# Strassen products for two column blocks of tiles 8 to 15, and a new order of all calls

## The reference, cut to what matters

```
x: (2, 1024, 2048) f32, ctx: (2, 2048, 2048) f32
q1 = fake_quant(layernorm(x)); q2 = fake_quant(ctx)     # (round(v/s + z) clipped to 0..255, - z) * s
x  = x + tanh(g_xattn) * (q1 @ q2)                      # main product, 1024 x 2048 x 2048 per batch
y  = layernorm(x)
logits = y @ route_w.T (8 experts); top-1 expert and its logit
h  = y @ A_e.T (rank 16); out = (logit * h of the top expert) @ Bw_e.T
x  = x + tanh(g_ffn) * out
```

## Time and profile before

| | |
|---|---|
| time of three runs | 363.27, 364.12, 364.35 us; median 364.12 |
| span of the profiled execution | 361.7 us, 2.4 us under the median |
| PE / DVE / ACT / POOL busy | 333.0 / 260.6 / 197.4 / 172.3 us |
| share of the span | 92 / 72 / 55 / 48 % |
| main matmuls of 512 columns, in the program | 1008, and 32 of 256 columns |

### The profile page before, as it was taken

How to read it: one execution, slowest core, us unless ns; L and a number is a source line. 1 busy time by engine, 2 the same in 40 slices (tenths; PEclk the granted TensorE clock), 3 DMA queues, 4 the chain that set the end, 5 groups by cost and what they waited for, 6 DMA issues and landing times.

```text
span 361.7 us, 5854 instructions
## 1 busy us (share of the span) xinstructions
PE 333.0 (92%) x2237; PEld 186.4 (52%) x2262; DVE 260.6 (72%) x553; ACT 197.4 (55%) x129; POOL 172.3 (48%) x199
## 2 busy tenths in 40 slices
PE   0389999999999999999998999999999999999983
PEld 0244454546756466455464546464464555465751
DVE  3855799898967896958658587945588567585853
ACT  1888489778967262747999270524062413204460
POOL 2559267431265162545999056627064441605281
PEclk9999999999999999999999999999999999999999
DMA  7999999895769998899799996666939890443956
GB/s 301 400 387 404 366 387 380 289 348 173 284 182 212 289 251 291 270 266 294 176 366 157 262 320 121 181 111 177 212 138 158 225 288 31 93 84 59 304 220 232
DMA packets 93906, 87.63 MB, mean 242 GB/s; under 512 B 71844, under 2 KB 72868, under 8 KB 89764
## 3 DMA queue, kind: packets, MB, share of 16 engines
q1 hardware_dynamic: 93856, 87.11, 79.5%
q10 hardware_dynamic: 12, 0.00, 0.0%
HBM read 52.49 MB, written 16.78 MB: 191 GB/s over the span
## 4 chain that ended last, share of the span: by engine, by line
PE 77%; DVE 8%; DMA 7%; issue 2%; ACT 2%; POOL 2%; ACTq 0%; SPq 0%; DVEq 0%
PE main L1575 46%; DMA xs<-in_x 4%; PE hp L1613 4%; PE hp L1617 4%; PE hp L1614 4%; PE outp L1575 4%; PE outp L1658 4%; PE outp L1660 3%; PE outp L1659 3%; DVE bn L971 3%; PE turn L1609 2%; DMA prow<-in_g_ffn 2%; DMA out<-xs 1%; ACT x L753 1%; PE turn L1503 1%
## 5 line engine op out<-in xcount | busy, mean ns | idle before, releaser
L1575 PE MATMUL main<-q,qa 128*128 128x512 bf16 x841 | 194.6, 380 | 5.0 <-POOL q L593 2.3
L1575 PEld LDWEIGHTS main<-q,qa 128*128 128x128 bf16 x864 | 83.2, 98 | 101.2 <-issue 2.7
L586 POOL TENSOR_TENSOR yn<-y,yn 128x2048 f16<-128x2048 f32 x13 | 53.0, 4077 | 31.7 <-ACT y L788 31.7
L735 ACT ACTIVATE c<-stage,zpc,inv 128x2048 int8<-128x2048 f32 x24 | 49.9, 2086 | 7.7 <-DMA stage<-in_ctx 4.0
L593 POOL CAST q<-c 128x2048 bf16<-128x2048 int8 x24 | 45.1, 1893 | 15.3 <-ACT c L735 14.8
L782 ACT ACTIVATE yn<-xs,sc 128x2048 f16<-128x2048 f32 x11 | 23.0, 2093 | 53.4 <-POOL sc L579 49.6
L1104 DVE SCALAR_TENSOR_TENSOR xs<-main,cc,xs 128x512 f32<-128x512 f32 x45 | 33.3, 740 | 21.7 <-PE main L1575 21.5
L574 POOL TENSOR_SCALAR ve<-mv 128x1 f32<-128x1 f32 x16 | 3.1, 191 | 84.8 <-DVE mv L1137 81.8
L1184 DVE SCALAR_TENSOR_TENSOR xs<-outp,tsc,xs 128x512 f32<-128x512 f32 x44 | 31.2, 735 | 13.6 <-PE outp L1660 13.5
L971 DVE BATCH_NORM_STATS2 bn<-xs 128x6 f32<-128x512 f32 x52 | 32.1, 680 | 10.6 <-DMA xs<-in_x 10.6
L753 ACT ACTIVATE x<-xs,sc 128x2048 int8<-128x2048 f32 x12 | 25.0, 2087 | 24.5 <-POOL sc L566 24.4
(11 more groups left out here) (132 smaller groups left out, 435.2 us busy)
## 6 DMA issues: line engine op xcount, KB each, us to landing
stage<-in_ctx SPq DMA_DIRECT2D x24, 1024.0 KB, 7.9
xs<-in_x SPq DMA_DIRECT2D x13, 1024.0 KB, 6.5
out<-xs SPq DMA_DIRECT2D x12, 1024.0 KB, 5.0
yT<-in_ctx SPq DMA_DIRECT2D x4, 1024.0 KB, 9.2
y<-in_ctx SPq DMA_DIRECT2D x4, 1024.0 KB, 10.1
c<-in_x SPq DMA_DIRECT2D x3, 1024.0 KB, 7.4
out<-c SPq DMA_DIRECT2D x3, 1024.0 KB, 7.3
c<-in_L_ffn_A SPq DMA_DIRECT2D x1, 1024.0 KB, 11.5
```

What stands on the lines that cost most here:

```text
L586: pool.tensor_tensor(yn[:, 1, :], y[:, :], yn[:, 0, :], ALU.subtract).then_inc(s_ylo_made, 1)
L735: act.activation(c8_of(piece), place(piece), ACT.Identity, bias=zpc[:, 1:2], scale=inv[:, 1:2])\
L1575: last = pe.matmul(bank_of(n)[:, :], q1T(t)[:, k, :], q2[:, nb, k, :], start=(k == 0), stop=(k == KC - 1))
```

## The change

Four things change.

First, the number formats: `q2`, `q1` and `qa`, and what transposes them, become f16 in place of bf16. All values are whole numbers of at most 128 in size, and sums of four of them stay exact in f16.

Second, tiles 8 to 15 are taken in pairs (8,9), (10,11), (12,13), (14,15). Column blocks 0 and 1 are still `main`. Blocks 2 and 3 of a pair are eight products of (128 rows x 1024 contracted) by (1024 x 512) before, and seven after, in the form of Strassen's scheme that shares sums. DVE makes four sums of halves of `q1T` for each pair (`make_sum`, 128x1024 f16, two SBUF operands), and once, for batch 1, four sums of the context (`make_t1` to `make_t4`, each in two halves of 128x2048 f16). A product is eight matmuls. Products 1, 6, 5, 3 run on in one PSUM bank (`turn0`), 7 and 4 in another (`turn1`), and 2 in a bank of `main`; DVE adds the bank to x after each, so that a pair has seven additions for these blocks instead of four, and PE may go on in a bank only when the addition has been made.

Third, buffers: `yn` holds one tile and not two; the low part of y is written over y itself (`y_low`), so `norm_full` of the next tile waits until `flip_low` has landed (`y_turned`). Tiles 11 and 12 have their homes in `stage`, since `c8` holds the context's sums. The last tile's y goes to `c8[0]`.

Fourth, all five lists are in a new order, in the first half too.

```diff
-HOME = [0, 7, 1, 2, 3, 4, 0, 1, 2, 3, 4, 6, 7, 0, 1, 2]
+HOME = [0, 7, 1, 2, 3, 4, 0, 1, 2, 3, 4, 8, 9, 0, 1, 2]
-        q2 = sb("q2", [P, NB, KC, NW], bf16)
+        q2 = sb("q2", [P, NB, KC, NW], f16)
-        yn = sb("yn", [P, 2, D], f16)
+        yn = sb("yn", [P, D], f16)
+        qs = sb("qs", [P, 3, HK, P], f16)
         def y_turned(t):
-            return s_ylo_made, YN.index(t) + 1
+            return s_yloT_loaded, 16 * (YN.index(t) + 1)
+ADDED = {1: (0, W0), 2: (0, W0), 3: (0, W0 + 1), 4: (1, W0), 5: (1, W0 + 1), 6: (1, W0), 7: (1, W0 + 1)}
+        def factor_b(i):
+            return {1: q2[:, W0, 0:HK, :], 2: q2[:, W0, HK:KC, :], 3: q2[:, W0 + 1, HK:KC, :], 4: c8h[2],
+                    5: c8h[1], 6: c8h[0], 7: q2[:, W0 + 1, 0:HK, :]}[i]
+        def factor_a(t, i):
+            return {1: q1T(t)[:, 0:HK, :], 2: q1T(t)[:, HK:KC, :], 3: qs[:, 1, :, :], 4: q1T(t + 1)[:, HK:KC, :],
+                    5: qs[:, 0, :, :], 6: qs[:, 1, :, :], 7: qs[:, 2, :, :]}[i]
+            def make_sum(t, j):                       # j = 1; 2, 3 and 4 alike
+                    dve.tensor_tensor(qs[:, 0, :, :], low[:, 0:HK, :], low[:, HK:KC, :], ALU.add)\
+                       .then_inc(s_sum_made[0], 1)
...
+            def make_t1(half):                        # make_t2, make_t3, make_t4 alike
+                dve.tensor_tensor(half_of(c8h[1], half), in_q2(LATE + half), in_q2(LATE - PIECES + half), ALU.subtract)\
+                   .then_inc(s_t1_made, 1)
...
+            def add_product(t, i):
+                n, (into, nb) = UNIT[t, f"m{i}"], block_of((t, f"m{i}"))
+                dve.wait_ge(s_main_done, n + 1)
+                dve.scalar_tensor_tensor(out=x_nb, in0=bank_of(n)[:, :], scalar=cc[:, :], in1=x_nb,
+                                         op0=ALU.mult, op1=ALU.add).then_inc(s_main_added, 1)
+                if COMPLETES[into, nb] == (t, f"m{i}"):
+                    bn_block(into, nb)
...
+            def product(t, i, run):
+                if run == 0:
+                    pe.wait_ge(s_main_added, bank_before(n) + 1)
+                for k in range(4 * run, 4 * run + 4):
+                    first = i in (1, 2, 7) and k == 0
+                    last = pe.matmul(bank_of(n)[:, :], factor_a(t, i)[:, k, :], factor_b(i)[:, k, :],
+                                     start=first, stop=(k == HK - 1), skip_group_check=i in (6, 5, 3, 4))
```

In DVE's list, from the first pair on:

```diff
+            make_sum(8, 1)
+            make_t1(0)
+            make_sum(8, 3)
+            make_sum(8, 2)
+            add_main(8, 1)
+            make_t1(1)
+            make_t3(0)
+            add_main(9, 0)
+            stats1(10)
+            add_main(9, 1)
+            add_product(8, 1)
+            make_t3(1)
+            make_t2(0)
+            make_t2(1)
+            make_t4(0)
+            make_sum(8, 4)
+            add_product(8, 2)
+            add_product(8, 7)
+            add_product(8, 6)
+            make_t4(1)
...
+            stats1(12)
+            make_sum(10, 1)
+            add_product(10, 1)
+            make_sum(10, 2)
```

In PE's list, the first pair:

```diff
+            product(8, 1, 0)
+            product(8, 1, 1)
+            product(8, 7, 0)
+            product(8, 2, 0)
+            product(8, 2, 1)
+            product(8, 7, 1)
+            product(8, 6, 0)
+            product(8, 6, 1)
+            h_rows_high(7)
+            h_rows_low(7)
+            expert_product(6, 3)
+            product(8, 4, 0)
+            product(8, 5, 0)
```

More of the change, by code:

```diff
@@ L268, in build @@
         turn = [bank("turn0"), bank("turn1")]
-        turnb = [t[:, :].bitcast(bf16) for t in turn]
+        turnb = [t[:, :].bitcast(f16) for t in turn]
         hp = bank("hp")
@@ L1873, in _ @@
             main(7, 0, 3)
+            h_rows_high(5)
+            h_rows_low(5)
+            main(7, 2, 0)
+            main(7, 1, 0)
+            main(7, 1, 1)
             main(7, 1, 2)
+            turn_wh(5)
+            main(7, 2, 1)
+            main(7, 2, 2)
             main(7, 1, 3)
-            main(7, 2, 0)
-            expert_product(4, 2)
-            main(7, 2, 1)
+            expert_product(5, 0)
+            expert_product(5, 1)
+            main(7, 2, 3)
+            column_sums(8, range(W0))
@@ new lines, in _ @@
+            product(8, 7, 0)
+            column_sums(8, range(W0, NB))
+            column_sums(9, range(W0, NB))
+            product(8, 2, 0)
[8 more added lines that the diff above has]
+            product(8, 5, 0)
+            product(8, 4, 1)
+            main(10, 0, 0)
+            main(10, 0, 1)
@@ L1935, in _ @@
+            main(10, 0, 2)
+            product(8, 5, 1)
+            main(10, 1, 0)
+            main(10, 1, 1)
+            turn_wh(7)
+            main(10, 1, 2)
             expert_product(7, 0)
+            product(8, 3, 0)
+            product(8, 3, 1)
             expert_product(7, 1)
+            expert_product(7, 2)
+            main(10, 0, 3)
+            main(10, 1, 3)
+            column_sums(10, range(NB))
+            expert_product(7, 3)
+            product(10, 2, 0)
+            product(10, 1, 0)
@@ L1937, in _ @@
+            product(10, 1, 1)
+            product(10, 2, 1)
+            column_sums(11, range(NB))
+            main(11, 0, 0)
+            main(11, 0, 1)
+            main(11, 0, 2)
+            product(10, 6, 0)
+            product(10, 6, 1)
+            main(11, 1, 0)
+            product(10, 7, 0)
+            product(10, 7, 1)
+            product(10, 5, 0)
+            product(10, 5, 1)
+            main(11, 1, 1)
             h_rows_high(8)
             h_rows_low(8)
-            expert_product(7, 2)
@@ L1958, in _ @@
-            main(10, 3, 3)
+            product(10, 4, 0)
+            product(10, 4, 1)
+            product(10, 3, 0)
+            product(10, 3, 1)
+            turn_wh(8)
+            main(11, 0, 3)
+            expert_product(8, 0)
+            expert_product(8, 1)
+            main(11, 1, 2)
+            main(11, 1, 3)
             h_rows_high(9)
+            main(12, 0, 0)
+            expert_product(8, 2)
             h_rows_low(9)
-            expert_product(8, 0)
-            column_sums(11, range(NB))
```

1159 lines of the change are left out of this document (618 added, 541 removed).

## The result

The changed kernel takes 385.18 us (median; 385.14 to 387.59) against 363.75 of the kernel before on the same chip: a ratio of 1.061, with an interval from 1.059 to 1.063. It is slower by 21.4 us. I had predicted 358.7.

The account below looks back on a forecast made before the run. The prediction took the sum of PE's work as the bound: 361.7 - 6.9 - 1.5 - 0.5 + 2.0 + 1.5 = 356.3 us of span, with 2.4 to the median 358.7 us; range 354.0 to 365.5.

Parts of the forecast that it names:

- The first half: Tiles before the pairs: work the same, an earlier load_x(2) gains a little; -0.5 us, between -2 and +1.5.
- the sign of it: Listed as showing the forecast wrong: PE idle before tile 8, caused by the first half's new order, costed at almost nothing.
- Matmuls: Blocks 2 and 3 of four pairs: 32 matmuls fewer at 0.216 us each, where PE has no idle time; -6.9 us.
- The stall at 190: Chain of store, load and DVE statistics near 190 us: taken as all gained, -1.5 us, 0 as the other end.
- Is DVE late?: Blocks (8,0) to (12,0): DVE has 74.8 us of work in about 77.5, holding PE +2.0 us, between 0 and 8.
- my walk: DVE's and PE's lists stepped through by price from the end of block (7,3): PE held at four places, 2.5 to 3 us.
- Two readers of SBUF: DVE's new sums meeting POOL's SBUF reads, two meetings up to 1.9 and 4.1 us: +1.5 us, between 0 and 6.
- rival C: Two-source sums run at one element per cycle, PE held about 10 us in the first pair: 368.7 us, slower; chance 0.12.
- A: Rival: DVE's overlap absorbs the holds but for 1.0 us and no sum meets POOL: 355.7 us; chance 0.28.
- B: Rival: gain goes into waits for DVE, POOL meetings recur in pair (12,13), transposes land late: 363.7 us, no change; chance 0.15.
- The y chain: norm_full's new wait for the tile before's landing, and flip_q1(9) behind load_ctx(31): both together 0, at worst 4 us.
- The tail: After the last main block: the same calls in nearly the same order, 0.

Follow-up runs that it names:

- e2: Changed kernel with the order of the kernel before on every engine to the end of tile 7; formats, buffers and products as changed: 378.55 us.
- e1: Changed kernel with each skipped column_sums call of tiles 0 to 3 spread to its own block, and unit_terms with them: 379.76 us.
- e9: Order of the kernel before to tile 11, seven products only in pairs (12,13) and (14,15), 16 matmuls fewer than before: 372.35 us.
- e19: Pairs-from-tile-12 kernel of 364.81 us with gate(10) ahead of a row sum and the last pair's product 3 addition ahead of an expert addition: 362.49 us.
- e8: Changed kernel with each matmul of the first product done twice, adding 32 matmuls (6.9 us): 386.92 us.
- e17: e16 with each matmul of the first product done twice, adding 16 matmuls (3.45 us): 371.13 us.
- e11: e9 with transposes of q ahead of flip_low, and gates and expert additions moved between products: 370.06 us.
- e14: Pairs-from-tile-12 kernel of 370.21 us with take_wh(10) ahead of affine_x(14) and gate(12) behind the additions of products 7 and 5: 368.31 us.
- e16: Pairs-from-tile-12 kernel of 364.46 us with make_t3 moved behind product 1, also make_t4(1), statistics of x(14) and x(15), and the last pair's product 4: 367.48 us.
- e3: Kernel before with f16 factors and y's low part kept in y, norm_full waiting for the transpose; no order changed: 363.74 us.
- e5: e2 with DVE's statistics of x(9) moved behind the expert additions that PE waited for: 379.33 us.

## Why the prediction was wrong, step by step

**The step that failed first: "The first half. Its work is the same", -0.5, between -2 and +1.5.** It measured +15.8 at the seventh gate, and 6.6 at the end (e2). I argued from the work, and the diff changes the order of every list there. The reason that I gave for looking no further, that PE has only 2.4 us of idle time to win from 50 to 190, bounds the gain and says nothing of the loss; I wrote "a bad order could lose some" and gave it no price. e1 shows 5.4 us of it (seven skipped calls in a row), e2 the rest of the 15.8 as order. The prediction has no term for the gathered calls of `column_sums`, nor for loads that now stand right ahead of transposes in SP's list. I did name the sign of it: idle time of PE before tile 8.

**The second half failed too, and it is the larger part.** My terms for it were -6.9 - 1.5 + 2.0 + 1.5 = -4.9 us. In e2, with a first half in the old order, it costs 14.7 us from the seventh gate to the last; in the changed kernel 5.7 us come on top of the 15.8. The step that failed is the overlap: I took a matmul out at its full price and let DVE hold PE for 2.0 us in all. What the runs show in its place is a row of waits of 1 to 6 us in tiles 8 to 15, and the slow clock behind some of them. That the order of the calls makes them is shown for the last two pairs, where e9 to e19 take them away; for the pairs (8,9) and (10,11) the cause stays open between the order and what DVE has to do there.

**"Matmuls", -6.9.** Right as work: 32 fewer. Wrong as time in this order: e8 gives 1.7 us for the same 6.9, by the intervals less than 5. It needs PE to be the bound, and e17 (3.65 for 3.45) shows that it holds where the order is near that of before. My premise, "as long as nobody else becomes late", was the whole matter.

**"The stall at 190", -1.5.** Failed, and I had named the wrong load. The one in the earlier trace rows brings `x(9)`, into the place that `store(4)` frees; `load_x(10)` waits for `store(5)`. The stall is still there in the changed kernel, ahead of `add_main(7, 1)` in DVE's list, and PE waits 1.4 us behind it, as it did before:

```profile
189.65 2.47 DVE L1030 BATCH_NORM_STATS2 bn<-xs 128x6 f32<-128x512 f32 x4 [3.39 <-DMA xs<-in_x]
```

With the first half restored, PE waits 7.2 us between 184 and 200 (e2), for additions behind the statistics of the same `x(9)`: the same form of chain, only longer.

**"Is DVE late?", +2.0, between 0 and 8.** The kind was right, the size too small, and my walk had ideal starting times. DVE is busy for 63.88 of the 70 us from 200 on, 91%, as I had said. PE's idle time from 200 to 350 is 9.3 us in the changed kernel against 0.7. Each kernel from e11 to e14 removed a wait and brought up one of 2 to 5.6 us elsewhere, among them one of a kind that my walk did not have: ACT's `take_wh` behind `affine_x`. DVE's total was near, 295.8 for 290, but the row sums alone took 20.2 us for my 10.5, by the meetings of the next step.

**"Two readers of SBUF", +1.5, between 0 and 6.** Right in mechanism, and inside the range; the term was too small. The longest row sums of the changed kernel, of 0.69 each when alone:

```profile
254.74 3.89 DVE L1181 TENSOR_TENSOR qs<-qs,qa 128x1024 f16<-128x1024 f16 x1
298.79 3.86 DVE L1191 TENSOR_TENSOR qs<-qa,qs 128x1024 f16<-128x1024 f16 x1
```

The first, `make_sum(10, 2)`, met POOL's `low_rows(8)`, which I had named with the sum ahead of it, and PE waited 3.2 us for it, twice my 1.5 for both meetings. e16 shows the same: 6.22 in place of 2.35. The rule of the Trainium skill (SBUF — State Buffer, Who interferes with whom), by which such a pair holds each other for the whole instruction, agrees with both: 254.74 + 3.89 is 0.6 us after POOL's subtraction ends (258.07), the length of one sum.

I also wrote that most context sums fall where POOL is idle. In the changed kernel they held POOL's `first_norm(10)`, an instruction of one element per partition with a median of 0.34:

```profile
223.62 3.42 POOL L627 TENSOR_SCALAR sc<-mv,sc,zpc 128x1 f32<-128x1 f32 x1
235.51 0.82 PE L1766 MATMUL main<-q,qa 128*128 128x512 f16 x3 [2.21 <-DMA qa<-q]
```

It stands in the chain that ended last: behind it come ACT's quantising (2.1), POOL's widening (1.9) and the transpose (4.25), for which PE waits 2.2 us. I had this meeting at nothing.

**The sums' rate; rival C.** Two groups that met nobody, by shape, us in total and mean ns of one:

```profile
L1186 DVE TENSOR_TENSOR qs<-qa 128x1024 f16<-128x1024 f16 x4 | 2.7, 668 | 1.5 <-issue 1.5
L1212 DVE TENSOR_TENSOR q<-q 128x2048 f16<-128x2048 f16 x2 | 2.4, 1216 | 0.0
```

0.67 and 1.22 us: two elements per cycle, as the casts to 16 bits had it and as the Trainium skill (VectorE: DVE Perf Modes, The perf-mode tier table) states with 1224 ns for 2048. C's mechanism did not occur. That the result lies beyond C's 368.7 is no support for it. Rivals A and B, which shared my first half, failed with it; and B, "the gain goes into waits", was the right kind of answer.

**"The y chain", 0, at worst 4.** 0 in the order of before (e3). In the new order PE waited 4.7 + 2.7 us for transposes of `y`, more than my worst, as they were issued late on SP.

**"The tail", 0.** Right: from the last gate's scaling to the end 11.8 us before and 12.0 after.

## What to carry to other kernels

When a diff takes work out and rewrites the order of in-order queues, the order is the larger change: price it first, everywhere that it differs, also where the arithmetic is the same, and do not read a small idle time as a bound on the loss. Test first whether removed work is worth anything by doing some of it twice; in the changed kernel 6.9 us gave 1.7, in the one near the old order 3.45 gave 3.65. It tells how much of PE's work counts, not what the change costs elsewhere. And make the change in the smallest stretch with the old order elsewhere; a collision removed shows the next one, so follow the waits until they are small.

## What the runs showed of the hardware

- Seven calls in a row whose branches are skipped cost PE a stop of 5.3 us that the profile puts down to "issue", and the clock of that stretch was 0.92; spread among matmuls they cost nothing visible, and it was 1.00 (e1).
- The issue of a transpose occupies SP: 34 of them take 80.1 us before, 2.4 each; in the changed kernel the seven that start within 2.2 us after SP has issued a load of 1 MB took 3.8 to 8.1.
- The hold between DVE and POOL goes both ways, also for the smallest instruction. In e5 this one, of 0.34 when alone, ran beside three f16 sums of DVE that follow each other, and ended with the third; it did not get in between them:

```profile
218.14 3.43 POOL L627 TENSOR_SCALAR sc<-mv,sc,zpc 128x1 f32<-128x1 f32 x1
218.03 2.35 DVE L1221 TENSOR_TENSOR c<-q,c 128x2048 f16<-128x2048 f16 x2
220.30 1.22 DVE L1229 TENSOR_TENSOR c<-q,c 128x2048 f16<-128x2048 f16 x1
```

- After a stop of 1 to 3 us, the next eight matmuls ran at 1.2 GHz in some places (3.46 us in e16) and at 2.4 in others: in the changed kernel at 258.77, behind a wait of 3.16, eight took 1.89.
